# Two attention layers with an MLP on one core: the orders around the first step, the end of cross attention and the tail

## What is computed

```python
ln_out = layernorm(hidden_states, ln1_s, ln1_b)
q, k, v = jnp.split(ln_out @ w_qkv + b_qkv, 3, axis=-1)
x = hidden_states + merge_heads(attention(q, k, v, ltor_mask)) @ w_ao + b_ao        # A
q = layernorm(x, ln2_s, ln2_b) @ w_q + b_q
k, v = jnp.split(encoder_states @ w_kv + b_kv, 2, axis=-1)
x = x + merge_heads(attention(q, k, v, cross_mask)) @ w_co + b_co                   # B
x = x + gelu(layernorm(x, ln3_s, ln3_b) @ w1 + b1) @ w2 + b2                        # MLP
# second layer, D: Q = x @ Wq.T, K and V from layernorm(audio_kv), no biases
x = x + jnp.tanh(gate) * (attention(Q, K, V, mask) @ Wo.T)
# attention: softmax(q k^T / sqrt(32) * mask - 10000 * (1 - mask)) v, per head
```

## Time and profile before

| | us |
|---|---|
| median of 3 runs | 1102.22 (1100.93 to 1102.42) |
| the profiled execution | 1104.91 |
| its span in the profile | 1103.5 |
| busy PE, DVE, ACT, POOL | 1074.2, 820.7, 713.3, 462.2 |

### The profile page before, as it was taken

How to read it: one execution, slowest core, us unless ns; L and a number is a source line. 1 busy time by engine, 2 the same in 40 slices (tenths; PEclk the granted TensorE clock), 3 DMA queues, 4 the chain that set the end, 5 groups by cost and what they waited for, 6 DMA issues and landing times.

```text
span 1103.5 us, 24330 instructions
## 1 busy us (share of the span) xinstructions
PE 1074.2 (97%) x8829; PEld 934.1 (85%) x8829; DVE 820.7 (74%) x1314; ACT 713.3 (65%) x2365; POOL 462.2 (42%) x337
## 2 busy tenths in 40 slices
PE   7989999999999999899999999999999999999998
PEld 6888888888888888787898888888888988888886
DVE  6678887778888777798877557656676478778777
ACT  4687777777788777687444434434445387777776
POOL 3665665657767776576612121103022331122100
PEclk9999999999999999999999999999999999999999
DMA  6356665577776777465241130220532146666533
GB/s 216 102 185 203 194 195 182 182 222 216 225 225 214 214 210 233 141 207 152 67 144 48 40 96 1 96 94 2 166 107 92 59 144 207 206 195 208 178 95 96
DMA packets 136136, 167.06 MB, mean 151 GB/s; under 512 B 16992, under 2 KB 82256, under 8 KB 136016
## 3 DMA queue, kind: packets, MB, share of 16 engines
q1 hardware_dynamic: 136016, 165.50, 48.5%
HBM read 113.15 MB, written 52.29 MB: 150 GB/s over the span
## 4 chain that ended last, share of the span: by engine, by line
PE 57%; DVE 12%; ACT 9%; DMA 8%; POOL 5%; issue 5%; SPq 4%; DVEq 0%; ACTq 0%
PE psum L930 15%; PE psum L911 14%; PE psum L750 12%; PE psum L850 5%; PE psum L744 5%; POOL prob L1995 4%; ACT prob L1207 4%; DMA normalised<-ln_tile 2%; ACT prob_blocks L1207 2%; PE psum L768 2%; PE psum L786 2%; DVE prob L1572 2%; PE psum L827 2%; DVE ln_tile L1510 2%; ACT inputs_transposed L1245 2%
## 5 line engine op out<-in xcount | busy, mean ns | idle before, releaser
L750 PE MATMUL psum<-inputs_hi,weights_hi 128*128 128x256 f32 x768 | 223.7, 291 | 5.0 <-POOL inputs_lo L1986 2.2
L750 PE MATMUL psum<-inputs_lo,weights_hi 128*128 128x256 f32 x768 | 217.1, 283 | 0.0
L750 PE MATMUL psum<-inputs_hi,weights_lo 128*128 128x256 f32 x768 | 217.0, 283 | 0.0
L1986 POOL TENSOR_TENSOR inputs_lo<-inputs_transposed,inputs_hi 128x512 fp32r<-128x512 f32 x84 | 112.4, 1359 | 240.8 <-DVE inputs_hi L1545 181.1
L1995 POOL TENSOR_TENSOR prob<-prob,mask_bias 128x1024 f32<-128x1024 f32 x64 | 153.2, 2417 | 96.4 <-DVE prob L1572 94.4
L1207 ACT ACTIVATE prob<-prob,negmax 128x128 f32<-128x128 f32 x472 | 182.3, 392 | 0.3 <-DVE negmax L1585 0.2
L750 PEld LDWEIGHTS psum<-inputs_hi,weights_hi 128*128 128x128 f32 x768 | 146.7, 191 | 10.3 <-issue 2.6
L1585 DVE TENSOR_REDUCE negmax<-prob 128x8 f32<-128x1024 f32 x96 | 115.8, 1209 | 47.2 <-POOL prob L1995 47.1
L750 PEld LDWEIGHTS psum<-inputs_lo,weights_hi 128*128 128x128 f32 x768 | 147.0, 191 | 0.2
L750 PEld LDWEIGHTS psum<-inputs_hi,weights_lo 128*128 128x128 f32 x768 | 146.9, 191 | 0.0
L850 PE MATMUL psum<-weights_hi,context_parts 128*128 128x512 f32 x376 | 125.5, 393 | 0.2 <-ACT kT L1158 0.2
(11 more groups left out here) (124 smaller groups left out, 2605.4 us busy)
## 6 DMA issues: line engine op xcount, KB each, us to landing
prob_turned<-prob_blocks SPq DMA_DIRECT2D x37, 512.0 KB, 3.0
prob<-prob_turned SPq DMA_DIRECT2D x148, 128.0 KB, 3.4
weights_whole<-weights_in SPq DMA_DIRECT2D x72, 256.0 KB, 3.4
normalised<-ln_tile SPq DMA_DIRECT2D x30, 512.0 KB, 2.8
inputs_transposed<-normalised SPq DMA_DIRECT2D x120, 128.0 KB, 2.9
context<-row_sums_spread SPq DMA_DIRECT2D x188, 64.0 KB, 2.1
stream<-residual SPq DMA_DIRECT2D x42, 256.0 KB, 2.8
residual<-stream SPq DMA_DIRECT2D x42, 256.0 KB, 3.8
```

Of the source, the lines that this page charges most:

```text
L750: mm = pe.matmul(ps[:, bank, GT * part:GT * part + GT], w[:, slot, c, o], a[:, buf, c, :], start=c == 0 and i == 0, stop=c == KC - 1 and i ...
L1986: pool.tensor_tensor(lo, y, hi.bitcast(f32), ALU.subtract).then_inc(s_rlo if fill.ln is None else s_flo, 1)
```

## The change

The kernel after computes the same with the same instructions; their places change, and four banks.

- **Start.** The first queries and keys (A, 0, 0 to 3) are projected into banks 0 to 3 instead of 6 and 7, without waits for what left those before. `project` waits for each weight chunk's `lo` part ahead of the chunk (`chunk_split`) and no longer for all first. On VectorE `first_hi(1)` goes one split earlier, `normalise(FILLS[1])` between the two splits of unit 1, and `normalise(FILLS[2])` behind both masks of step 0. TensorE does half of step 0's first projection ahead of `scores(0)`. In step 1 `inverse_sums(0)` goes ahead of `turn_inputs`, and `fill_hi` ahead of `normalise(FILLS[3])`.
- **End of cross attention.** SP in step 27: `load_transposed` ahead of `load_tiles`. Steps 28 and 29 on VectorE: `row_max` and `prob_out(27,3)` ahead of `turn_inputs` in 28, `statistics` behind the maxima, `turn_inputs` ahead of the maxima in 29. ScalarE: `prob_out` ahead of the fill, in 28 also the first quarter of the exponentials. POOL in 28: residual and `inverse_deviation` ahead of `fill_lo`. Steps 30 and 31: on VectorE `inverse_sums` and `context_lo` ahead of the masks; on ScalarE `context_hi(29)` between the exponentials of step 30. `w2(1)` in two parts, one to each side of `times_v(31)`.
- **MLP.** Unit 15 is split (ScalarE and POOL) at (0, 5) ahead of the fill, and not at (0, 6).
- **Tail.** On VectorE `prob_out(46,1)` ahead of `mask_scores(47,1)`, `prob_out(46,3)` ahead of `row_max(47,1)`, `stream(45)` behind `context(46)`.

```diff
@@ -193,7 +193,9 @@
-    return PLACE[phase, q, n] % 2 if (phase, q, n) in PLACE else n % 2
+    if (phase, q) == (A, 0) and n < 4:
+        return n
+    return 6 + (PLACE[phase, q, n] % 2 if (phase, q, n) in PLACE else n % 2)
@@ -603,12 +605,14 @@
                     store_normalised(st.ahead)
-                if st.later and st.later.ln is not None and ahead_ln:
+                if st.later and st.later.ln is not None and ahead_ln and g != 27:
                     load_tiles(st.later)
...
                     load_transposed(st.ahead)
+                if g == 27:
+                    load_tiles(st.later)
                 if st.phase == B and st.b == 13:
@@ -712,6 +716,13 @@
+            def chunk_split(unit, c):
+
+                if (unit, c) in LO_COUNT_DVE:
+                    pe.wait_ge(s_wlod, LO_COUNT_DVE[unit, c])
+                else:
+                    pe.wait_ge(s_wlo, LO_COUNT[unit, c])
+
             def project(phase, q, n, bank, parts=(0, 1)):
@@ -729,24 +740,21 @@
                         pe.wait_ge(s_rlo, 2 * raw_fill(D, q, 0).n + last + 1)
-                    if q == 0:
-                        if (unit, KC - 1) in LO_COUNT_DVE:
-                            pe.wait_ge(s_wlod, LO_COUNT_DVE[unit, KC - 1])
-                        else:
-                            pe.wait_ge(s_wlo, LO_COUNT[unit, KC - 1])
-                        if unit == 1:
-                            pe.wait_ge(s_wlod, LO_COUNT_DVE[1, 1])
                 for part in parts:
...
                             for i, (a, w) in enumerate(((xhi, whi), (xhi, wlo), (xlo, whi))):
+                                if q == 0 and i == 0:
+                                    chunk_split(unit, c)
                                 mm = pe.matmul(ps[:, bank, :], a[:, buf, c, tok], w[:, slot, c, :],
...
                             for i, (w, a) in enumerate(((whi, xhi), (whi, xlo), (wlo, xhi))):
+                                if q == 0 and i == 0:
+                                    chunk_split(unit, c)
                                 mm = pe.matmul(ps[:, bank, GT * part:GT * part + GT], w[:, slot, c, o], a[:, buf, c, :],
@@ -911,7 +919,7 @@
-            def w2(p):
+            def w2(p, tiles=None):
                 group, j = group_of(p)
@@ -919,7 +927,7 @@
                     pe.wait_ge(s_wlo, max(LO_COUNT[W2_UNIT[n], c] for c in range(KC)))
-                for t in group_tiles(group):
+                for t in tiles or group_tiles(group):
                     if j == 0 and group.first == 0:
@@ -930,7 +938,8 @@
                                            stop=j == NPAIR * group.stretches - 1 and e == chunks - 1 and i == 2)
-                mm.then_inc(s_w2, 1)
+                if tiles != (0,):
+                    mm.then_inc(s_w2, 1)
@@ -951,10 +960,14 @@
                     times_v(g - 2)
-                scores(g)
+                if g:
+                    scores(g)
+                else:
+                    project(*st.units[0], U_BANK, (0,))
+                    scores(g)
                 if was and (was.units[2] or was.units[0]):
                     half_out(*(was.units[2] or was.units[0]))
-                project(*st.units[0], U_BANK)
+                project(*st.units[0], U_BANK, (0, 1) if g else (1,))
                 if late:
@@ -1023,8 +1036,9 @@
                 transpose_prob(31, 3)
+                w2(1, (0,))
                 times_v(31)
-                w2(1)
+                w2(1, (1,))
                 project_out(31)
@@ -1097,20 +1111,16 @@
             first_values()
-            half_out(A, 0, 4)
-            project(A, 0, 0, U_BANK)
-            half_out(A, 0, 5)
-            project(A, 0, 1, U_BANK + 1)
+            project(A, 0, 0, S_BANK)
+            project(A, 0, 1, S_BANK + 1)
             fill_transpose(FILLS[1])
-            half_out(A, 0, 0)
-            project(A, 0, 2, U_BANK)
-            half_out(A, 0, 1)
-            project(A, 0, 3, U_BANK + 1)
+            project(A, 0, 2, S_BANK + 2)
+            project(A, 0, 3, S_BANK + 3)
             for phase in (A, B):
...
                     if phase == A and i == 0:
-                        half_out(A, 0, 2)
-                        half_out(A, 0, 3)
+                        half_out(A, 0, 4)
+                        half_out(A, 0, 5)
                     if phase == A or st.b < 14:
@@ -1145,7 +1155,7 @@
                 name, half = HALVES[phase][n]
-                gp, bank = q % 2, U_BANK + unit_bank(phase, q, n)
+                gp, bank = q % 2, unit_bank(phase, q, n)
                 turn = 8 * phase + q
@@ -1164,7 +1174,7 @@
                 half = HALVES[D][n][1]
-                bank = U_BANK + unit_bank(D, q, n)
+                bank = unit_bank(D, q, n)
                 turn = 16 + q
@@ -1325,13 +1335,18 @@
                     probs_out(g - 1)
+                if g in (28, 29):
+                    prob_out(g - 1, 2)
+                if g == 28:
+                    exps(g, 0)
                 if st.fill in TURNED:
                     fill_out(st.fill)
-                if st.prev and g - 1 in BY_PE:
+                if st.prev and g - 1 in BY_PE and g not in (28, 29):
                     prob_out(g - 1, 2)
...
                     half_out(*st.units[2])
-                exps(g, 0)
+                if g != 28:
+                    exps(g, 0)
                 exps(g, 1)
@@ -1344,9 +1359,10 @@
                     g = 16 + b
-                    context_hi(g - 2, 0)
-                    context_hi(g - 2, 1)
-                    if b == 15:
+                    if b == 14:
+                        context_hi(g - 2, 0)
+                        context_hi(g - 2, 1)
+                    else:
                         tanh(0)
@@ -1358,6 +1374,9 @@
                     exps(g, 2)
+                    if b == 14:
+                        context_hi(29, 0)
+                        context_hi(29, 1)
                     exps(g, 3)
@@ -1460,14 +1479,13 @@
                 if (g, jp) == (0, 5):
+                    for c in range(KC):
+                        split((15, c))
                     fill_scale(mlp_fill(1))
...
                     fill_scale(FILLS_OF_MLP[g][1])
-                if (g, jp) == (0, 6):
-                    for c in range(KC):
-                        split((15, c))
                 if (g, jp) == (7, 0):
@@ -1618,7 +1636,7 @@
                     return
-                bank = U_BANK + unit_bank(phase, q, n)
+                bank = unit_bank(phase, q, n)
                 turn = 8 * phase + q
@@ -1708,13 +1726,16 @@
                 mask_scores(g, 1)
+                if g == 0:
+                    normalise(FILLS[2])
                 if late:
...
                     context_lo(g - 2, 1)
+                if st.prev and not st.ends:
+                    inverse_sums(g - 1)
                 if g == 1:
...
                 if st.prev and not st.ends:
-                    inverse_sums(g - 1)
                     row_max(g, 0)
@@ -1726,21 +1747,30 @@
                     normalise(st.ahead)
-                if st.ends or not st.prev:
+                if g == 28:
+                    row_max(g, 0)
+                    prob_out(g - 1, 3)
+                    turn_inputs(st.fill)
+                    row_max(g, 1)
+                    statistics(st.ahead)
+                elif g == 29:
+                    turn_inputs(st.fill)
+                    row_max(g, 0)
+                elif st.ends or not st.prev:
                     row_max(g, 0)
...
                         turn_inputs(st.fill)
-                    if st.ahead == mlp_fill(0):
-                        statistics(st.ahead)
                 if st.units[2]:
                     v_out(*st.units[1])
-                if g != 33:
+                if g not in (28, 33):
                     row_max(g, 1)
-                if st.prev and g - 1 in BY_PE and g != 33:
+                if st.prev and g - 1 in BY_PE and g not in (28, 33):
                     prob_out(g - 1, 3)
+                if g == 1:
+                    fill_hi(st.fill)
                 if ahead_ln and not later_ln and st.ahead != mlp_fill(0):
                     normalise(st.ahead)
-                if st.fill and st.fill.ln is not None:
+                if st.fill and st.fill.ln is not None and g != 1:
                     fill_hi(st.fill)
@@ -1762,12 +1792,15 @@
                     context(g - 2, 1)
+                    if b == 14:
+                        inverse_sums(g - 1)
+                    context_lo(g - 2, 0)
+                    context_lo(g - 2, 1)
+                    if b == 15:
+                        inverse_sums(g - 1)
                     make_mask_bias(g)
...
                     mask_scores(g, 1)
-                    inverse_sums(g - 1)
-                    context_lo(g - 2, 0)
-                    context_lo(g - 2, 1)
                     prob_out(g - 1, 1)
@@ -1824,15 +1857,15 @@
                 row_max(47, 0)
+                prob_out(46, 1)
                 mask_scores(47, 1)
```

(18 more changed lines are left out.)

## The result

The changed kernel takes 1107.7 us in the median of its runs, the kernel before 1102.42 beside it: a ratio of 1.0043 over all runs of both (the two medians alone would give 1.0048), 95% interval 1.0035 to 1.0052. It is 0.43% slower; the forecast was 1101.8 and the range ended at 1104.8. One execution of a later kernel, e4, ran at a granted clock of 0.557, took 1761.76 us and is left out of its ratio.

A forecast was written before the change was run, and what follows sets the result against it. TensorE, busy 97% of the span, was taken as the bound, with time to win only in its stalls. Terms +2.1 - 2.2 - 0.6 + 0.25 = -0.45: 1104.5 us profiled, 1101.8 on the median's scale; range 1096.0 to 1104.8.

The forecast's parts named there:

- The collision and its chain: Start: normalising caught between POOL's additions ends at 42.2, tiles land at 48.4, inverse_sums(0) is done at 52.4.
- The start as a whole: Start: all its parts together cost +2.1 us, with bounds of -2.5 and +3.4.
- A shift made there stays: Start: all later loops depend on it, so its shift lasts unless a later wait swallows it.
- The end of cross attention, -2.2: Steps 27 to 31: reordering there gains 2.2 us, within a range of 2.9 to 0.7.
- 3.5 ahead at `row_sums(29)`: Steps 27 to 29: shorter waits put TensorE 3.5 us ahead when it reaches row_sums(29).
- nearer the free end, because one of the two has room: Steps 30 and 31: of normalise(mlp_fill(1)) and gelu_hi(0), one can be late harmlessly, so -2.2 us was taken.
- my own condition for 0.7: End of cross attention: the gain shrinks to 0.7 us if both operations meet unit 12's splits and the residual.
- The MLP's first steps, -0.6: MLP steps 5 and 6: splitting unit 15 ahead of the fill shortens two stalls, -0.6 us (0 to -1.0).
- The tail, +0.25: Tail: VectorE's new order adds a wait for the fourth transpose, +0.25 us (-0.4 to +0.4).
- my -0.45: Whole kernel: the sum of start, end of cross attention, MLP and tail, -0.45 us.
- (c): Slower rival: +3.4 at the start, collisions of gelu and MLP normalising; +2.75 in all, 1105.0 us; chance 0.15.
- Its late `inputs_transposed`: Step 2 on SP, in the slower rival: this late load also delays the probability blocks, start +3.4 us.

The follow-up runs named there:

- e4: The changed kernel with VectorE's order at the tail put back: ratio 1.0023 to the kernel before.
- k10: The changed kernel, order kept, seven eighths of step 0's mask additions on POOL left out and two splits of unit 3 moved later: ratio 1.0015.
- k7: The kernel before with one edit, normalise(FILLS[2]) behind step 0's masks: ratio 1.0033.
- k12: The kernel before with TensorE's part of the start alone (banks 0 to 3, chunk_split, half a projection ahead of scores(0), first_hi(1) earlier): ratio 0.9989.
- e2: The changed kernel with normalise(FILLS[2]) put back ahead of step 0's masks, fill_hi still ahead of normalise in step 1: ratio 0.9991.
- the second pair: A further execution of the changed kernel and of the kernel before, both unchanged: spans 1107.8 and 1102.1 us, ratios 1.0037 and 1.0001.
- k8: The kernel before with the change at the end of cross attention alone: ratio 0.9994.
- k6: The changed kernel with stream(29), context(30) and inverse_sums(31) ahead of tanh_argument(1) and the gelu parts behind it on VectorE in step 31: ratio 1.0018.
- e1: The changed kernel with normalise(FILLS[2]) back ahead of step 0's masks and fill_hi back behind normalise in step 1: ratio 1.0003.
- k15: The kernel before with the MLP's edit alone, unit 15 split in step 5 ahead of the fill: ratio 1.0003.
- e3: The changed kernel with fill_hi put back behind normalise in step 1, masks still ahead of normalising in step 0: ratio 1.0037.
- k16: The kernel before with the tail's VectorE orders alone: ratio 1.0011.
- k9: The changed kernel with 35 idle transposes before row_sums(0) and 18 before row_sums(31), into banks meant to be free: ratio 1.0056.
- k5: The changed kernel with 34 idle transposes before row_sums(0) and 18 before row_sums(31), into the bank row_sums writes next: ratio 1.0052.

## Why the prediction was wrong

Of the terms of the sum, the start came out as forecast. The end of cross attention, which was to pay for it, was taken at the wrong end of its own range, and the two small terms were taken too well.

**The collision and its chain: right.** Normalising caught behind both additions, the late landing, `rtotal` near 52, `v_out` behind 2.9 us of normalising: each row came within 0.7 us of its forecast. k10 shows POOL's additions as the cause, k7 that the one order is enough. This also bears out the sentence of the Trainium skill ("SBUF — State Buffer", "Who interferes with whom") by which I called masks first a bad order. The start as a whole was forecast at +2.1, and two pairs of executions have +2.4 and +2.7. Its two halves by times: TensorE's part -1.2 (k12), masks first +3.6 (k7) and +5.7 (e2 against the changed kernel), where my working had 4.6 between a collision and none. The half clock behind the wait isn't in my working at all.

**"A shift made there stays": right** in the second pair (+0.1 up to scores(27)). In the first 1.5 us of it went, which the second doesn't repeat.

**The end of cross attention, -2.2: the step that failed.** Its first half was right: "3.5 ahead at `row_sums(29)`" is 3.7 in the mean of the executions. Its second half was not. I let 3.5 shrink to between 2.9 and 0.7 and wrote "I take -2.2, nearer the free end, because one of the two has room": it shrinks to 0.7 by k8's times (1.3 by the traces), the worst end. The step that failed is that choice. In the changed kernel's trace both operations do meet unit 12's splits and the residual on POOL, which was my own condition for 0.7. `normalise(mlp_fill(1))`:

```profile
486.36 2.44 DVE L1528 TENSOR_SCALAR ln_tile<-ln_tile,ln_mean_var,ln_rstd 128x512 f32<-128x512 f32 x2
```

It took 1.01 in the kernel before. This one did have room: VectorE waits 1.1 us for exponentials behind it. The other had none. VectorE from 500 us on, and POOL:

```profile
500.81 1.28 DVE L1670 SCALAR_TENSOR_TENSOR kT<-kT,qT 128x512 f32<-128x512 f32 x1
502.12 1.40 DVE L1678 TENSOR_SCALAR hidden_parts<-kT 128x512 fp32r<-128x512 f32 x1
503.56 0.69 DVE L1682 SCALAR_TENSOR_TENSOR hidden_parts<-kT,hidden_parts 128x512 fp32r<-128x512 f32 x1
504.17 1.78 DVE L1687 SCALAR_TENSOR_TENSOR kT<-kT,qT 128x512 f32<-128x512 f32 x1
505.87 0.68 DVE L1658 TENSOR_TENSOR residual<-psum,residual 128x512 f32<-128x512 f32 x1
506.47 0.74 DVE L1627 TENSOR_TENSOR context<-psum,context 128x256 f32<-128x256 f32 x2
507.13 0.24 DVE L1611 RECIPROCAL rtotal<-total 128x16 f32<-128x16 f32 x1
```

```profile
498.99 2.54 POOL L1994 TENSOR_TENSOR weights_lo<-weights_whole,weights_hi 128x512 fp32r<-128x512 f32 x2
501.49 1.75 POOL L2031 TENSOR_TENSOR residual<-residual,bias_rows 128x512 f32<-128x512 f32 x1
504.10 1.29 POOL L2031 TENSOR_TENSOR residual<-residual,bias_rows 128x512 f32<-128x512 f32 x1 [0.86 <-DMA residual<-stream]
```

And the same two operations of `gelu_hi(0)` in the kernel before:

```profile
503.22 0.82 DVE L1652 SCALAR_TENSOR_TENSOR kT<-kT,qT 128x512 f32<-128x512 f32 x1
504.07 0.43 DVE L1660 TENSOR_SCALAR hidden_parts<-kT 128x512 fp32r<-128x512 f32 x1
```

`gelu_hi(0)` takes 1.4 us longer, as I had priced. What I never priced is the next one: I didn't follow VectorE's queue on to `inverse_sums(31)`, and `tanh_argument(1)` met POOL's second addition for another 1.1 us. The exponentials ended at 505.22 and their inverse began at 507.13. TensorE, 3.7 us early, waits 2.3 us for it, where the kernel before waited 0.5. k6 moves the inverse ahead of `tanh_argument(1)` and is 0.0025 below the changed kernel, 2.8 us, with some 1.6 to either side. In e1 and k10 the second addition came too late for that meeting, and only 0.9 and 1.0 us are lost instead of 1.9 to 3.7. So this part of the price depends on a landing, and it fell on the bad side in six of eight executions.

**The MLP's first steps, -0.6: too much.** k15 has +0.3 by its times, whose interval (-1.0 to +1.8 us) still takes in -0.6, and -0.1 by its waits. The fill behind the splits made `context_parts` 0.3 us later, where I had counted that wait as gone.

**The tail, +0.25: right against one trace, too small against ten.** TensorE's end stands 21.6 us behind scores(47) in eight of ten profiled executions with the new order. The kernel before's first has 21.3, but the ten with the old order have 20.8 to 21.4, 21.1 in the mean. So the new order costs 0.5 us there. In two executions with the new order, e2 and e3, the clock fell behind the wait of 1.5 us for `scale_rows`, and it was 22.9 and 22.8. e2's row:

```profile
1090.00:1092.00 2.00, 2.00 (x22) 1.34 (x20) 0.61 (x1) 0.00 (x0) 0.00 (x0) 0.50 0.42 116
```

With the old order, whose longest wait there is 0.8 us, none of ten fell. In the mean that adds 0.3 us, 0.7 in all. k16's +1.2 (with 1.2 to either side) agrees with that.

**The sum again, by times.** TensorE's start -1.2, masks first +3.6, end of cross attention -0.7, MLP +0.3, tail +1.2: +3.2, with an error of about 2.7 (five intervals of about 1.2 each, added in squares); measured are 4.1 and 4.7. `fill_hi` first and `inverse_sums(0)` first aren't in this sum. Against my -0.45 the end of cross attention makes 1.5 of the difference, the MLP 0.9, the tail up to 1.0 and the start the rest. One pair of executions, at +1.0, would have hidden most of the loss; the means over many showed it.

**The rivals.** (c), 1105.0, came nearest, for half of its reason: the gelu and the MLP's normalising did collide with POOL, and its -0.7 at the end of cross attention is what k8 measured. Its late `inputs_transposed` isn't seen. It got 0.15, too little: I tied the two prices together, though the second alone would have moved the sum from -0.45 to +1.05.

## What to carry to other kernels

When a change brings an engine 3 us ahead, ask for each of its next waits what the releasing engine still has queued at that time, down to the smallest operation: here a reciprocal of 0.24 us, behind a gelu and a tanh argument that POOL had held up for 2.5 us, took back most of the gain. Where a price lies between two ends by a collision that can't be excluded, the near end isn't the likeliest; and where one side of the collision waits for a landing, executions of one kernel fall on both sides. Before an experiment is read as clean, look whether the thing that it removes had happened in its trace at all. An order that releases another engine's long SBUF operations just ahead of one's own short SBUF operation costs at the next dependent load, not where it stands: here one moved line, 3.6 to 5.7 us.

## What the runs showed of the hardware

TensorE's granted clock fell to 0.5 (1.2 GHz) at each of the six waits of 3.8 to 4.4 us before `row_sums(0)` and at each of the six of 2.3 us before `row_sums(31)`, for 3.41 us. In k6 and k7 it was 6.83 us, from within waits of 4.4 and 3.8. It also fell after waits of 2.4 us (k15), 2.1 (k9), 1.7 (e1) and, in two of ten executions, 1.5 (the tail). It stayed after one of 2.3 us in k10 and after most of 1.5 to 2.0 us. k5, which filled most of its two long waits with idle transposes, has full clock over its whole span. Of e1's, at 58.6, nothing was left at scores(4), behind the next waits; in the tail, where TensorE's own work sets the end, it cost 1.2 to 1.3 us. The last store (128 KB) landed after 1.7 to 2.0 us in ten executions and after 2.7 to 3.7 in the other ten, with either order. VectorE's normalising of two tiles took 1.0 us alone, 1.96 beside a POOL subtraction and 4.7 to 4.9 between two POOL additions of 2.4 us.
